# The second half of an MLP stage: one running sum over three groups of columns for three nested branches

## What is computed

```python
def _mlp_branch(xp, w1, b1, w2, b2, keep_ch):
    cmask = (jnp.arange(C) < keep_ch)
    h = jax.nn.gelu(xp * cmask @ w1 + b1, approximate=False)
    return (h @ w2 + b2) * cmask
m_large = _mlp_branch(nl2, w_fc1, b_fc1, w_fc2, b_fc2, C)
m_small = sum(gumbel_weights[i] * _mlp_branch(ns2, w_fc1, b_fc1, w_fc2, b_fc2, C // (i + 1)) for i in range(3))
```

## Time and profile before

| | |
|---|---|
| median of 3 runs | 1053.75 us (1049.52 to 1054.3) |
| the profiled execution | 1050.69 us, span 1049.0 us |
| PE busy | 913.2 us, 87% of the span |
| DVE, ACT, POOL busy | 53%, 43%, 39% |
| mean granted TensorE clock | 0.93 of full speed |
| the MLP stage | from about 473 to 615 us of the span |
| TensorE in part 1 | from some 533.5 to 612.4 us |

### The profile page before, as it was taken

How to read it: one execution, slowest core, us unless ns; L and a number is a source line. 1 busy time by engine, 2 the same in 40 slices (tenths; PEclk the granted TensorE clock), 3 DMA queues, 4 the chain that set the end, 5 groups by cost and what they waited for, 6 DMA issues and landing times. The chain is left out here.

```text
span 1049.0 us, 20975 instructions
## 1 busy us (share of the span) xinstructions
PE 913.2 (87%) x7607; PEld 803.0 (77%) x7607; DVE 554.0 (53%) x1446; ACT 449.2 (43%) x1099; POOL 405.7 (39%) x443
## 2 busy tenths in 40 slices
PE   7979999999974898983999979888879998999885
PEld 6868898888973777763999966776669997767674
DVE  2215555455555776656643236877734333555474
ACT  1235555555532666642344417666613122444320
POOL 4534443343443222224322135757730471333341
PEclk9989999999995999995999978999956999999998
DMA  9901101111100000005000002521100121222251
GB/s 288 281 24 37 27 23 31 39 32 28 43 1 5 14 18 9 19 9 165 1 1 1 1 24 58 124 59 36 38 1 1 47 80 52 77 77 75 60 163 45
DMA packets 54819, 55.51 MB, mean 53 GB/s; under 512 B 20064, under 2 KB 45008, under 8 KB 54720
## 3 DMA queue, kind: packets, MB, share of 16 engines
q1 hardware_dynamic: 48800, 42.00, 14.6%
q0 software_dynamic: 3792, 7.84, 2.2%
q10 hardware_dynamic: 2128, 4.34, 1.4%
HBM read 29.61 MB, written 13.92 MB: 42 GB/s over the span
## 5 line engine op out<-in xcount | busy, mean ns | idle before, releaser
L688 POOL TENSOR_TENSOR attn_prob<-attn_prob,attn_recip 100x432 f32<-100x432 f32 x64 | 58.4, 912 | 117.5 <-DVE attn_recip L1046 117.5
L814 PEld LDWEIGHTS psum<-attn_prob_t,attn_values 108*64 108x64 f32 x1024 | 66.9, 214 | 26.5 <-issue 14.1
L814 PE MATMUL psum<-attn_prob_t,attn_values 108*64 108x36 f32 x1024 | 73.9, 291 | 12.7 <-issue 5.6
L237 POOL TENSOR_TENSOR attn_prob_x<-attn_prob,attn_recip 100x864 f32<-100x864 f32 x32 | 52.6, 1644 | 72.2 <-DVE attn_recip L519 72.2
L1484 POOL DMA_INDIRECT results<-moe_hid_shared x43 | 41.2, 959 | 87.9 <-ACT moe_hid_shared L1669 87.9
L1041 DVE TENSOR_REDUCE attn_row_sum<-attn_prob 100x12 f32<-100x432 f32 x64 | 38.4, 600 | 55.4 <-ACT attn_prob L913 55.1
L1260 ACT ACTIVATE mlp_hid<-psum,columns 128x384 f32<-128x384 f32 x72 | 40.0, 581 | 57.4 <-PE psum L78 39.4
L1644 ACT ACTIVATE moe_silu<-psum 128x384 f32<-128x384 f32 x36 | 17.7, 490 | 72.3 <-PE psum L78 72.3
L788 PE MATMUL psum<-attn_keys_a,attn_q_a 128*64 128x288 f32 x256 | 47.4, 447 | 0.0
L2018 PE MATMUL psum<-embed_w_tok,embed_patches 128*128 128x192 f32 x216 | 40.1, 346 | 8.4 <-DMA embed_w_tok<-in_tok_w 5.7
L1169 POOL TENSOR_TENSOR mlp_rstd<-mlp_var_eps,neg_half 128x1 f32<-128x1 f32 x18 | 10.6, 588 | 92.0 <-DVE mlp_var_eps L1315 92.0
(11 more groups left out here) (384 smaller groups left out, 2900.7 us busy)
## 6 DMA issues: line engine op xcount, KB each, us to landing
embed_patches<-in_x SPq DMA_DIRECT2D x18, 384.0 KB, 23.8
sorted_rows<-mlp_pad_rows SPq DMA_DIRECT2D x1, 4214.0 KB, 16.8
moe_hid_shared<-sorted_rows SPq DMA_DIRECT2D x43, 98.0 KB, 1.9
attn_v<-attn_v_tok SPq DMA_DIRECT2D x16, 216.0 KB
attn_values<-attn_v_tok SPq DMA_DIRECT2D x96, 27.0 KB
raw_a<-in_w_gu_dram SPq DMA_DIRECT2D x8, 288.0 KB, 3.1
raw_b<-in_w_gu_dram SPq DMA_DIRECT2D x16, 144.0 KB, 3.4
h_rows<-results SPq DMA_DIRECT2D x6, 288.0 KB, 5.5
```

Source lines behind the costliest of these rows:

```text
L237: nc.gpsimd.tensor_tensor(prob_x[k % 2][:, :, :, :], prob[k % 3][:, :, :].rearrange("p h (a n) -> p h a n", a=1) .to_broadcast([QP, HEADS, ...
L688: nc.gpsimd.tensor_tensor(pr, pr, recip[k % 2][:, :].rearrange("p (h a) -> p h a", a=1) .to_broadcast([QP, HEADS, SEQ]), ALU.mult).then_in ...
L814: last = nc.tensor.matmul(ps[r:r + 64, n // 2, a * SEQ:(a + 1) * SEQ], v[:, n, :], prob_t[k % 2][:, n, a, :], start=True, stop=True)
```

## The change

In part 1 each chunk of hidden units keeps its bank for three steps. Step n belongs to group `n % 9 // 3` and chunk `3 * (n // 9) + n % 3`: three chunks take features 0 to 63 (group 0), then the same three add features 64 to 95 (group 1), then features 96 to 191 (group 2), then the other three chunks do so. After each step a gelu reads the bank, for the branch that keeps 64, 96 and 192 features in turn, and the next group's matmuls add to the same sum. Groups take two, one and three matmuls. For that, parts of x and of the weights are laid side by side in other partitions: `w_first`, `w_mid`, `w_last_hi` and `w_last_lo` are copied by VectorE after the post-norms of iterations 0 and 1 (`arrange_weights`), with zeros from GpSimd; `round_x` takes three activations and two copies, and `split_groups` two affine operations and four subtractions, with a signal for each group. The down products of three steps form a group; they follow one place behind the ups, the last group of an iteration behind the first three ups of the next. Step 0 writes with `start=True` from a weight padded to 192 columns. Part 0 is as before but for `arrange_weights`.

```diff
+        x_mid = sb("x_mid", [TILE, MW], F32R)
+        w_first, w_mid = sb("w_first", [P, HID], F32R), sb("w_mid", [TILE, HID], F32R)
+        w_last_hi, w_last_lo = sb("w_last_hi", [P, HID], F32R), sb("w_last_lo", [P, HID], F32R)
+        w_dn_pad = sb("w_dn_pad", [P, D])
...
+        def group_of(n):
+            return n % 9 // 3
+
+        def chunk_of(n):
+            return 3 * (n // 9) + n % 3
+
+        def cols_of(n):
+            return slice(chunk_of(n) * P, chunk_of(n) * P + P)
+
+        def hid_step(n):
+            return hid[n // chunks % 2][:, n % chunks, :]
+
+        def rounded_before(i):
+            return 2 * min(i, share) + 5 * max(0, i - share)
...
+            for w in (w_last_hi, w_last_lo):
+                nc.gpsimd.memset(w[:, :].bitcast(F32), 0.0).then_inc(S["zeros_ready"], 1)
+            nc.gpsimd.memset(w_dn_pad[:, :], 0.0).then_inc(S["zeros_ready"], 1)
             over_iterations(pool, body)
...
             def body(part, j, following):
-                branches = len(parts[part][0])
+                if part == 1:
+                    return nested_body(j, following)
                 up(part, j, 0)
-                for br in range(1, branches):
-                    up(part, j, br)
-                    down(part, j, br - 1)
+                transpose_x(part * share + j + 1)
+                down(part, j, 0)
+
+            def up_step(j, n):
+                i, first = share + j, before(1, j)
+                if n == 0:
+                    pe.wait_ge(S["x_first_split"], j + 1)
+                    pe.wait_ge(S["gelu_done"], first)
+                    if j == 0:
+                        pe.wait_ge(S["weights_arranged"], 9)
+                elif n >= 3:
+                    pe.wait_ge(S["gelu_done"], first + n - 2)
+                if n == 3:
+                    pe.wait_ge(S["x_mid_split"], j + 1)
+                    pe.wait_ge(S["x_rounded"], rounded_before(i + 1))
+                if n == 6:
+                    pe.wait_ge(S["x_split"], i + 1)
+                group, out, cols = group_of(n), bank(n % 3)[:, 0:MW], cols_of(n)
+                if group == 0:
+                    nc.tensor.matmul(out, w_first[:, cols], xs.b[:, :], start=True, stop=False,
+                                     skip_group_check=True)
+                    last = nc.tensor.matmul(out, w_up.a_lo[0:DB, cols], xs.b[0:DB, :], start=False, stop=False, skip_group_check=True)
+                elif group == 1:
+                    last = nc.tensor.matmul(out, w_mid[:, cols], x_mid[:, :], start=False, stop=False, skip_group_check=True)
+                else:
+                    nc.tensor.matmul(out, w_last_hi[:, cols], xs.a_hi[:, :], start=False, stop=False, skip_group_check=True)
+                    nc.tensor.matmul(out, w_last_hi[:, cols], xs.a_lo[:, :], start=False, stop=False, skip_group_check=True)
+                    last = nc.tensor.matmul(out, w_last_lo[:, cols], xs.a_hi[:, :], start=False, stop=True, skip_group_check=True)
+                last.then_inc(S["up_done"], 1)
+
+            def down_step(j, n):
+                i, steps = share + j, per_iter[1]
+                pe.wait_ge(S["gelu_done"], before(1, j) + n + 1)
+                if n == 0:
+                    pe.wait_ge(S["mlp_added"], 3 * i)
+                    if j == 0:
+                        pe.wait_ge(S["down_scaled"], 4)
+                w = w_dn_pad[:, :] if n == 0 else w_dn_s[2 - group_of(n)][:, chunk_of(n), :]
+                for t in range(3):
+                    last = nc.tensor.matmul(bank(3 + t)[:, 0:w.shape[1]], hid_step(n)[:, t * MT:(t + 1) * MT], w,
+                                            start=(n == 0), stop=(n == steps - 1))
+                    if n == steps - 1:
+                        last.then_inc(S["down_done"], 1)
+
+            def down_group(j, k):
+                for n in range(3 * k, 3 * k + 3):
+                    down_step(j, n)
...
+            def nested_body(j, following):
+                for k in range(6):
+                    for n in range(3 * k, 3 * k + 3):
+                        up_step(j, n)
+                    if k == 0 and j > 0:
+                        down_group(j - 1, 5)
+                    elif 1 <= k < 5:
+                        down_group(j, k - 1)
                 if following:
-                    transpose_x(part * share + j + 1)
-                down(part, j, branches - 1)
+                    transpose_x(share + j + 1)
+                down_group(j, 4)
+                if not following:
+                    down_group(j, 5)
...
             def round_x(part, j):
                 act.wait_ge(S["x_transposed"], part * share + j + 1)
                 ga, gb, ba, bb = parts[part][2]
+                if part == 1:
+                    mid = slice(DB, TILE)
+                    nc.scalar.activation(xs.b[0:DB, :], bank(6)[0:DB, 0:MW], ACT.Identity, bias=ba[0:DB, :],
+                                         scale=ga[0:DB, :]).then_inc(S["x_rounded"], 1)
+                    nc.scalar.activation(xs.a_hi[DB:P, :], bank(6)[DB:P, 0:MW], ACT.Identity, bias=ba[DB:P, :],
+                                         scale=ga[DB:P, :]).then_inc(S["x_rounded"], 1)
+                    nc.scalar.activation(xs.a_hi[0:DB, :], bank(7)[0:DB, 0:MW], ACT.Identity, bias=bb, scale=gb
+                                         ).then_inc(S["x_rounded"], 1)
+                    act.wait_ge(S["x_rounded"], rounded_before(part * share + j) + 2)
+                    for at in (0, DB):
+                        nc.scalar.activation(x_mid[at:at + 32, :], xs.a_hi[mid, :], ACT.Copy
+                                             ).then_inc(S["x_rounded"], 1)
+                    return
...
-                    c = n % chunks
-                    nc.scalar.activation(hid[(n // chunks) % 2][:, c, :], bank(n % 3)[:, 0:MW], ACT.Gelu,
+                    c = chunk_of(n) if part == 1 else n
+                    nc.scalar.activation(hid_step(n), bank(n % 3)[:, 0:MW], ACT.Gelu,
...
+            def split_groups(i, ga, gb, ba, bb):
+                done, mid = rounded_before(i), slice(DB, TILE)
+                dve.wait_ge(S["x_rounded"], done + 2)
+                nc.vector.tensor_scalar(x_aff_a[:, :], bank(6)[:, 0:MW], ga, ba, ALU.mult, ALU.add
+                                        ).then_inc(S["x_affine"], 1)
+                dve.wait_ge(S["x_affine"], 2 * i + 1)
+                nc.vector.tensor_tensor(xs.b[DB:P, :], x_aff_a[0:DB, :], xs.b[0:DB, :].bitcast(F32), ALU.subtract
+                                        ).then_inc(S["x_first_split"], 1)
+                nc.vector.tensor_tensor(x_mid[32:DB, :], x_aff_a[mid, :], xs.a_hi[mid, :].bitcast(F32), ALU.subtract
+                                        ).then_inc(S["x_mid_split"], 1)
+                dve.wait_ge(S["x_rounded"], done + 3)
+                nc.vector.tensor_scalar(x_aff_b[:, :], bank(7)[0:DB, 0:MW], gb, bb, ALU.mult, ALU.add
+                                        ).then_inc(S["x_affine"], 1)
+                nc.vector.tensor_tensor(xs.a_lo[DB:P, :], x_aff_a[DB:P, :], xs.a_hi[DB:P, :].bitcast(F32),
+                                        ALU.subtract)
+                dve.wait_ge(S["x_affine"], 2 * i + 2)
+                nc.vector.tensor_tensor(xs.a_lo[0:DB, :], x_aff_b[:, :], xs.a_hi[0:DB, :].bitcast(F32),
+                                        ALU.subtract).then_inc(S["x_split"], 1)
...
                 post_norm(i, 2)
+                if i < 2:
+                    arrange_weights(i)
+
+            def arrange_weights(i):
+                mid, end = slice(DB, TILE), slice(TILE, P)
+                copies = [(w_first[0:DB, :], w_up.a_hi[0:DB, :]), (w_first[DB:P, :], w_up.a_hi[0:DB, :]),
+                          (w_mid[0:32, :], w_up.a_hi[mid, :]), (w_mid[32:DB, :], w_up.a_hi[mid, :]),
+                          (w_mid[DB:TILE, :], w_up.a_lo[mid, :])]
+                if i == 1:
+                    dve.wait_ge(S["zeros_ready"], 2)
+                    copies = [(w_last_hi[0:DB, :], w_up.b_hi[0:DB, :]), (w_last_hi[end, :], w_up.a_hi[end, :]),
+                              (w_last_lo[0:DB, :], w_up.b_lo[0:DB, :]), (w_last_lo[end, :], w_up.a_lo[end, :])]
+                for to, view in copies:
+                    nc.vector.tensor_copy(to, view).then_inc(S["weights_arranged"], 1)
 
             pre_norm(0)
             split_x(0, 0)
             for n in range(3):
                 nc.vector.tensor_scalar(w_dn_s[n][:, :, :], w_dn[:, :, 0:D // (n + 1)], g[:, n:n + 1], None,
                                         ALU.mult).then_inc(S["down_scaled"], 1)
+            dve.wait_ge(S["zeros_ready"], 3)
+            dve.wait_ge(S["down_scaled"], 3)
+            nc.vector.tensor_copy(w_dn_pad[:, 0:D // 3], w_dn_s[2][:, 0, :]).then_inc(S["down_scaled"], 1)
```

(9 more changed lines are left out.)

## The result

Twenty runs of each kernel on one chip gave a median of 1060.78 us for the changed kernel (1052.78 to 1068.98) and of 1051.6 us for the kernel before (1047.37 to 1055.91): a ratio of 1.0088, 95% interval 1.0071 to 1.0105. The change costs 9.2 us. That is inside the range of 1051 to 1064 and 2.8 us from the 1058 forecast, but it is slower by more than 0.5%: the case that the prediction held likeliest, no difference that can be told (0.52), did not come; slower had 0.41. In the form of the prediction the sum was +4.4, and the chip says +9.2.

A forecast was written before the change was run, and what follows sets the result against it. TensorE was taken to bound the stage's second half, VectorE's chain the first half's two gaps. Second half -6.1 and first half +10.5 us gave +4.4: 1055.1 for the profiled execution, 1058 for the median, range 1051 to 1064.

The forecast's parts named there:

- Term 1: Up matmuls of the second half: 90 fewer in three iterations at 0.177 us each, -15.9 us.
- term 4: Handover of x, twice: TensorE stalls 0.9 us each because less work covers the split, +1.8 us.
- term 5: Handover of the down banks, twice: stall of 2.1 us each behind the residual adds, +4.2 us (2.5 to 5).
- term 6: Stage's end: third residual add starts some 1.95 us after TensorE's end, 0.13 before the change; +1.8 us.
- term 2: Down products of the second half: step 0 uses the padded 192-wide weight instead of 64-wide, +1.0 us.
- term 3: First second-half iteration: steps 3-5 wait for gelus emptying their banks, no down group between, +1.0 us (0 to 1.5).
- Term 7: First half: VectorE's weight copies delay the pre-norm, the first copy of a set waiting for GpSimd's addition; +6.9 us.
- Terms 8 and 9: First half: TensorE's clock falls after the longer gaps, +3.1 us; GpSimd's memsets delay x_hat at stage start, +0.5 us.
- The half clock reaches further: Slower rival: the clock also drops at the second half's handovers and costs more at first-half gaps; +9.0, 1063 us; chance 0.36.
- The copies at half rate: Slower rival: VectorE's weight copies run at half the assumed rate, 9.9 for 6.9 us, total 1061 us; chance 0.05.
- the waits that hide: Faster rival: copies start before GpSimd, clock as before, x_hat slips in, adds keep up; -6.1, 1048 us; chance 0.07.
- gelu as the pace: Rival: no TensorE time saved because gelu, 10.4 us of an iteration's about 21, becomes the pace; excluded unless the order clogs.

The follow-up runs named there:

- full_rows: Changed kernel, but the second matmul of group 0 takes all 128 rows instead of 64 (wrong sum); ratio 1.0052 to the kernel before.
- regrouped: Changed kernel, but in group 0 the three 128-row matmuls come first, then the three 64-row ones; ratio 1.01 to the kernel before.
- alternate: Kernel before, but in the 64-feature branch the middle matmul of three takes 128 rows; ratio 1.0151 to the kernel before.
- early_copies: Changed kernel, nine weight copies on ScalarE at the stage's start, clearing after GpSimd's first residual; ratio 0.9993 to the kernel before.
- all_three: Changed kernel with early ScalarE copies, last down group tile by tile, group 0's second matmul zero-padded to 128 rows; ratio 0.9909 to the kernel before.
- arrange_alone: Kernel before plus the new tiles, three memsets, nine copies and padding copy, read by nothing; ratio 1.0107 to the kernel before.

## Why the prediction was right or wrong

**Term 1 failed, by its price.** "90 fewer in three iterations, at 0.177 us: -15.9" is true of the 90 that went. It takes for granted that the 108 that stay cost what they did, and 36 of them (group 0) do not: 18 pairs of 128 and 64 rows at 0.37 a matmul. That is some +6.4 (6.9 if all 36 changes cost 0.19), shown by full_rows (away with equal rows), regrouped (two thirds of it away with a third of the changes left) and alternate (there without the change). The prediction's rows, have no such change, but the profile before does: the up steps of the 64-row branch stand between down products of 128 rows, two changes in an iteration. TensorE's weight load idles without a shown cause at just these six places of the second half (waits of the kernel before: us in total, times, longest):

```profile
PEld psum L1227 <- issue: 0.7, 3, 0.3
...
PEld psum L83 <- issue: 0.7, 3, 0.2
```

Some 0.23 us each, not all of which shows in the matmuls' starts. So the price could have been bounded before the change was timed: 36 changes at 0.23 are 8.3 us, an upper estimate. The Trainium skill (TensorEngine Tiling (Array Packing), "Key Properties") says "Mode switching requires drain", where 64 and 128 rows are two tiling modes. The runs agree, if these plain 64-row matmuls count as that mode, which no run shows by itself, and give the price that the page lacks, 0.19 us for each change. 96 and 128 rows mix without one: in the kernel before, an up matmul of 128 rows at 538.67 is followed by one of 96 at 538.85, the usual 0.18.

**Terms 4 to 6 hold, and the sum of 2 to 6 with them.** With term 1's miss taken out, the second half was forecast at 73.0 and full_rows has 72.0. The handover of x was 0.77 and 0.76 for 0.9 (term 4), the one of the banks 1.92 for 2.1 (term 5; 1.49 in one place behind half clock), and the third add at the end starts 1.95 after TensorE for 1.95 (term 6: 627.86 against 620.81 + 5.10, DVE row below). Padded products (term 2) and the gelus of the first iteration (term 3) were not tried by themselves. In the trace three padded products take 1.05 us (575.53 to 576.58) and six 64-wide ones 1.26, which makes term 2 +1.3 for +1.0. The first three steps of group 1 take 1.02 us (545.10 to 546.12) where they take 0.67 later (557.03 to 557.70), +0.35 for term 3's +1.0: the slow group 0 ahead of them gives the gelus time.

```profile
627.86 0.35 DVE L1420 TENSOR_TENSOR h_rows<-psum,mlp_residual 128x192 f32<-128x192 f32 x1
```

**Term 7 was right to half a microsecond, for a reason slightly off.** The copies cost 7.4 for 6.9, and the gaps grew by 4.03 and 3.31. One copy in each set does wait for GpSimd, at 1.66 for the 1.57 forecast, but it is the second. The Trainium skill's rule (SBUF — State Buffer, "SBUF: two separate sides"), that the shared ports are held for a whole instruction, agrees with the trace; what I drew from it, that a copy which starts first costs nothing, holds for that copy alone. The next in line pays, so the 2.0 us less were not there. GpSimd's addition lost too, 1.78 for 1.43. early_copies shows that no other part of the kernel had to hold these copies where they were.

**Terms 8 and 9.** Behind the first gap the transposes and down products took 1.34 + 6.85 us where the kernel before took 0.71 + 7.70, 0.2 less; behind the second it was 1.33 + 7.88 for 0.71 + 6.02, 2.5 more: +2.3 for +3.1. The third x_hat did slip in behind the first memset (476.44 + 8.32 = 484.76, the memset ends at 484.64), so the start gained 0.6 where a loss of 0.5 was forecast, and 0.7 more came from dense work that reached the full clock sooner after the start (490.12 to 498.18 for 489.59 to 498.37). The sum of the first half is 4.0 + 3.3 + 2.3 - 0.6 - 0.7 = 8.3, the measured 68.74 - 60.46, for a forecast 10.5.

**The sum, and the luck in it.** First half +8.3 (for +10.5). Second half, without any clock loss, -0.9 to -0.2 (for -6.1), and some 1.7 for each 3.4 us at half clock. With one such stretch that is 8.3 - 0.2 + 1.7 = 9.8 near the median's 9.2; the profiled execution, with four times that, was 14.0 above its counterpart before. The direction and the waits were worked out; that the time lies in the range although term 1 missed some 6.4 us is in part luck: the first half came 2.2 cheaper than forecast, and the range had been widened upward for the half clock; the forecast alone had 1053 to 1060, and the median is 1060.78.

**The rivals.** The half clock reaches further named +9.0 and a place, the handovers, and both are found in the traces; 13.6 us at half clock in one, 3.4 in the other. But the sum it was put on was too low by the rows, so its number was met mainly by another way, which no rival had: the matmuls that remain becoming dearer. Nor do two of the three falls in the first trace stand where it put them: at 566.3 and 597.1 the clock fell ahead of the long waits (ended at 575.53 and 603.90), behind the 0.77 for x and matmuls of group 0; the third came at the end of the wait of 1.92. The fall needs no row change: in full_rows, which has none in these steps, 10.2 us of the second half are at half clock, with the waits of 1.92 still there. Nor does it need a wait of PE: in alternate it fell where PE waited for nothing and only the weight loads stood idle. It stayed away in all_three, which had neither changes nor waits above 0.77. The copies at half rate, the waits that hide and gelu as the pace did not come.

Left open: the 3 us that arrange_alone and regrouped cost beyond their stage, and what decides in which executions the clock falls at a handover.

## What to carry to other kernels

When a change cuts matmuls, price the pattern that remains, not only what goes: on TensorE, look at the row counts of neighbours in the order of issue, and keep them alike, with zeros below if need be, since here 128 rows took no longer than 64 (0.17 to 0.18 us). Look for idle weight loads in the profile before: they had the price of the new pattern in them. One-time preparation belongs on the engine that stands idle at the stage's start, never between the two steps of a chain that another engine waits for. A saving that looks like nothing in total may be a real one with several prices on it: here -15.9 us was paid for by rows, waits and copies, each removable with a few lines, and 0.9% was left.

## What the runs showed of the hardware

- Where fp32r matmuls of 384 columns alternate between 64 and 128 rows they start 0.37 us apart, not 0.177, in either direction; 18 pairs cost some 6.4 us. 96 next to 128 rows costs nothing (0.18).
- The weight load shows it: idle 0.19 us before each such load, and 0.23 at each of the six changes in the kernel before.
- The granted clock can fall while PE is shown as 100% busy: 7.00 of 7.00 us before the fall in alternate, PEld 4.18 of 7.00.
- A VectorE copy of 768 columns takes 0.54 to 0.56 us with 32 or 64 partitions; one that stands behind GpSimd's addition takes 1.66, even where the copy before it began first.
- ScalarE takes 0.84 us for the same 768 columns, half as long again, and it was free at that time.
